# A new layout for the scratch that carries the query and key parts from one arrangement to another

## The reference

```python
def proj(W):
    return (X @ W.T).reshape(b, n, H, 2 * dh).transpose(0, 2, 1, 3)
Q, K, V = (proj(Wq), proj(Wk), proj(Wv))
Q1, Q2 = jnp.split(Q, 2, axis=-1)
K1, K2 = jnp.split(K, 2, axis=-1)
A1 = jnp.where(causal, jnp.einsum('bhnd,bhmd->bhnm', Q1, K1) * scaling, -jnp.inf)
A2 = jnp.where(causal, jnp.einsum('bhnd,bhmd->bhnm', Q2, K2) * scaling, -jnp.inf)
attn = jax.nn.softmax(A1, axis=-1) - lam * jax.nn.softmax(A2, axis=-1)
```

## Time and profile before

| | us |
|---|---|
| median of 3 runs | 543.09 |
| lowest and highest | 539.36, 544.16 |
| the profiled execution | 540.0 |
| its span in the profile | 538.0 |
| PE busy | 483.7 (90%) |
| DVE busy | 392.4 (73%) |
| ACT busy | 288.0 (54%) |
| POOL busy | 267.0 (50%) |

### The profile page before, as it was taken

How to read it: one execution, slowest core, us unless ns; L and a number is a source line. 1 busy time by engine, 2 the same in 40 slices (tenths; PEclk the granted TensorE clock), 3 DMA queues, 4 the chain that set the end, 5 groups by cost and what they waited for, 6 DMA issues and landing times.

```text
span 538.0 us, 8610 instructions
## 1 busy us (share of the span) xinstructions
PE 483.7 (90%) x3104; PEld 232.8 (43%) x3104; DVE 392.4 (73%) x796; ACT 288.0 (54%) x460; POOL 267.0 (50%) x223
## 2 busy tenths in 40 slices
PE   4892788888999999998997999999997998999995
PEld 4641443443445354453344545444343444443442
DVE  2414741969988988659887888469988977876584
ACT  1431444146686553656674654647773485548732
POOL 6031313124584914617653357626656467438963
PEclk9997789999999999999999999999999999999999
DMA  8700489803068480202486146111485166202111
GB/s 282 262 2 19 119 121 127 144 7 101 1 161 101 106 113 5 78 21 60 117 128 117 40 63 96 43 60 40 136 138 85 25 106 114 79 5 79 40 39 41
DMA packets 48474, 46.03 MB, mean 86 GB/s; under 512 B 5200, under 2 KB 38064, under 8 KB 47792
## 3 DMA queue, kind: packets, MB, share of 16 engines
q1 hardware_dynamic: 48432, 45.48, 41.0%
HBM read 37.47 MB, written 7.60 MB: 84 GB/s over the span
## 4 chain that ended last, share of the span: by engine, by line
PE 56%; DVE 15%; DMA 7%; SPq 7%; POOL 5%; ACT 4%; issue 4%; POOLq 1%; DVEq 0%; ACTq 0%
PE bank L737 7%; PE bank L728 6%; PE bank L749 6%; DMA ka<-parts_scratch 6%; PE scores L769 5%; SPq L514 5%; DVE nmax L1271 5%; PE scores L763 4%; PE bank L824 4%; PE scores L679 3%; PE scores L702 2%; PE scores L655 2%; PE scores L664 2%; PE scores L658 2%; PE bank L837 2%
## 5 line engine op out<-in xcount | busy, mean ns | idle before, releaser
L1070 POOL TENSOR_TENSOR gb<-gb,wb 128x512 f32<-128x512 f32 x64 | 84.7, 1324 | 114.8 <-ACT gb L978 104.2
L1271 DVE TENSOR_REDUCE nmax<-scores 128x4 f32<-128x1024 f32 (+1 forms) x96 | 113.7, 1216 | 32.2 <-PE scores L769 31.7
L1063 POOL TENSOR_SCALAR_AFFINE_SELECT pk<-pk 128x512 f32<-128x512 f32 (+1 forms) x96 | 82.9, 872 | 62.3 <-ACT pk L991 61.5
L991 ACT ACTIVATE pk<-scores 128x1024 f32<-128x1024 f32 x96 | 95.6, 1024 | 27.3 <-PE scores L769 27.1
L975 ACT ACTIVATE gt<-bank,bgh 128x512 f32<-128x512 f32 (+1 forms) x68 | 46.8, 688 | 62.6 <-PE bank L728 54.7
L737 PE MATMUL bank<-xnt,wu 128*128 128x512 f32 x128 | 69.2, 622 | 2.4 <-DVE h L1250 2.4
L728 PE MATMUL bank<-xnt,wg 128*128 128x512 f32 x128 | 68.7, 618 | 0.0
L749 PE MATMUL bank<-h,wd 128*128 128x512 f32 x128 | 66.8, 615 | 0.1
L1243 DVE SCALAR_TENSOR_TENSOR h<-gt,gb 128x512 f32<-128x512 f32 x64 | 49.6, 775 | 17.1 <-POOL gb L1070 12.6
L1250 DVE SCALAR_TENSOR_TENSOR h<-bank,bu,h 128x512 f32<-128x512 f32 x64 | 48.1, 751 | 17.3 <-PE bank L737 15.4
L763 PE MATMUL scores<-mask_h,ident_h 64*128 64x256 bf16 (+2 forms) x384 | 37.5, 273 | 12.3 <-DMA ka<-parts_scratch 8.2
(11 more groups left out here) (191 smaller groups left out, 732.3 us busy)
## 6 DMA issues: line engine op xcount, KB each, us to landing
wb<-wt_scratch SPq DMA_DIRECT2D x64, 256.0 KB, 4.1
parts_scratch<-parts SPq DMA_DIRECT2D x48, 128.0 KB, 2.4
qa<-parts_scratch SPq DMA_DIRECT2D x16, 192.0 KB
ka<-parts_scratch SPq DMA_DIRECT2D x16, 192.0 KB
qa<-parts_scratch SPq DMA_DIRECT2D x16, 128.0 KB
ka<-parts_scratch SPq DMA_DIRECT2D x16, 128.0 KB
x<-in_x SPq DMA_DIRECT2D x4, 256.0 KB, 2.7
ha<-in_wkq SPq DMA_DIRECT2D x1, 1024.0 KB, 5.2
```

The source lines that it names most:

```text
L991: A(dst.rearrange("p (h m) q -> p m h q", m=2), pairs[pair_of(step)][:, :, :].rearrange("p m (h q) -> p m h q", q=cols), ACT.Exp, scale=SC ...
L1063: pool.affine_select(out=dst, in_=dst, compare_op=ALU.is_ge, fill=0.0, base=0, pattern=[[0, heads], [1, P]], channel_multiplier=-1).then_i ...
L1070: pw(gb[:, c % 2, :], gb[:, c % 2, :], wb[:, k % 2, j % 2, :], ALU.mult).then_inc(s_ga_done, 1)
L1271: V.tensor_reduce(dst, src, AX, ALU.max, negate=True).then_inc(s_nmax_done, 1)
```

## The change

The scratch was laid out by chunk, q or k, head, component, term, dimension, token. It is now by chunk, q or k, batch, term, component, dimension, head, token. So the 16 heads x 256 tokens that a row of `qa` or `ka` takes lie in one run of 8 KB, where they were 16 runs of 512 B. For this the columns of `wq1` and `wk1` are put in order on the host, component first, then dimension, then head, so that tile f of a product holds component f. A tile that is stored is 128 rows of two runs of 512 B (one for each batch), where it was 128 rows of one run of 1 KB.

```diff
@@ step store
                                     r = a if n == 0 else 2 - a
                                     sp.wait_ge(done, at(c, name, 2 * n + f + 1))
-                                    dst = t["parts_dram"][c, n, f * 2 * GH:(f + 1) * 2 * GH, :, r * DH:(r + 1) * DH, :]
-                                    sp.dma_start(dst, parts[:, a, 2 * n + f, :]).then_inc(s_parts_stored, 16)
+                                    dst = t["parts_dram"][c, n, :, r, f * DH:(f + 1) * DH, :, :]
+                                    sp.dma_start(dst.rearrange("b d h t -> (d h) b t"),
+                                                 parts[:, a, 2 * n + f, :].rearrange("p (b t) -> p b t", b=CB)).then_inc(s_parts_stored, 16)
@@ step fetch
                                 for width in (3, 2, 1):
                                     first = 0 if n == 0 else 3 - width
-                                    src = t["parts_dram"][c, n, :, m, first * DH:(first + width) * DH, b * SEQ:(b + 1) * SEQ]
-                                    sp.dma_start(dst[row:row + width * DH, b, :, :],
-                                                 src.rearrange("h r t -> r h t")).then_inc(s_qk_in[b], 16)
+                                    src = t["parts_dram"][c, n, b, first:first + width, m * DH:(m + 1) * DH, :, :]
+                                    sp.dma_start(dst[row:row + width * DH, b, :, :], src).then_inc(s_qk_in[b], 16)
                                     row += width * DH
@@ the scratch
-    t["parts_dram"] = nc.dram_tensor("parts_scratch", (CHUNKS, 2, HEADS, 2, 3 * DH, CHUNK), BF16, kind="Internal").ap()
+    t["parts_dram"] = nc.dram_tensor("parts_scratch", (CHUNKS, 2, CB, 3, 2 * DH, HEADS, SEQ), BF16, kind="Internal").ap()
@@ the host
+    def rooms(w):
+
+        return w.reshape(P, HEADS, 2, DH).transpose(0, 2, 3, 1).reshape(P, -1)
-        "wq1": v["L1_attn_Wq"].T, "wk1": v["L1_attn_Wk"].T, "wv1": v["L1_attn_Wv"].T,
+        "wq1": rooms(v["L1_attn_Wq"].T), "wk1": rooms(v["L1_attn_Wk"].T), "wv1": v["L1_attn_Wv"].T,
```

## The result

The changed kernel takes 595.78 us (median of 4 runs, 594.58 to 596.47) against 543.62 us: a ratio of 1.097 with a 95% interval of 1.092 to 1.102. It is 52 us slower. I had said 30, with an upper end of 590: the way was right, the size and the range were not.

The account below looks back on a forecast made before the run. PE was taken to bound the kernel, five of eight fetches ending on its path. 27.1 + 1 + 1 + 4 - 3 = 30.1 us on 540.0 gave 570.1, plus 3 for the median: 573, range 555 to 590.

Parts of the forecast that it names:

- The mechanism: Fetches of ka: the smaller slowest count sets the engines, so the three DMA kinds use 3, 2 and 8.
- the five fetches on the path: Fetches 0/0, 1/0, 2/0, 3/0 and 3/1, each longer microsecond being one of PE's: +27.1 us together.
- the two with cover: Fetches 1/1 and 2/1, which had 24.2 and 24.3 us and need 23.5 to 24.5: +1 us for both.
- the stores: Stores to the scratch: 256 runs of 512 B for 128 of 1 KB, still 16 engines, +1 us.
- the clock: PE at half clock after four long waits, half of it counted: +4 us, between 0 and 14.
- the time of a fetch: Two engines carry 68 rows, 21.5 us at 25.9 GB/s, plus 2.0 fixed: 23.5 us from first issue.
- What comes back: Other engines drain their work while PE waits, so PE's idle 10% shrinks: -3 us, between 0 and -6.
- (c): Rival: wb parts queue behind fetches on the two engines, POOL's product L1070 waits longer, 585 to 590 us; chance 0.11.
- (a): Rival: fetches stay spread over the engines and long runs pay, so all four PE waits go, about 535 us; chance 0.06.
- (b): Rival: fetches stay spread but run length was never the limit, so nothing changes, 543 us; chance 0.09.

Follow-up runs that it names:

- the bare transfers: No kernel, only DMAs of 8 KB rows, each kind four times: 24 rows from 3 x 8 took 10.62 us, plain 24 rows 5.05 us.
- e1: Changed kernel with component ahead of term in the scratch, so a fetch's source rows lie together: 534.79 us, 0.981 of the original; second run 535.47 us, 0.979.
- e5: Changed kernel with 60 of the 64 wb loads left out: 578.89 us, ratio 1.065 to the kernel before the change.
- e4: Changed kernel with idle matmuls in front of PE's waits for the fetches: 586.72 us, ratio 1.076 to the kernel before the change.

## Why the prediction went wrong in size

- **The mechanism was right.** The source's 3 and 2 set the engines., one DMA of 24 KB, carried this; the shares 0.18 and 0.12 of the bare transfers and the 0.13 of the fetch show it, and e1 undoes it alone.
- **The sum.** In place of 27.1 for the five fetches on the path, 1 for the two with cover, 1 for the stores, 4 for the clock and -3, together 30.1, the profiles show 41.8 + 3.8 + 12.1 - 1.9 = 55.8; what the stores did is in the 41.8.
- **The step that failed first: the time of a fetch.** I took 23.5 us plus what lies ahead, 121.3 us for the five; they took 136.9, 15.6 more. I counted what the two engines have ahead, not what runs beside them: the `wb` loads that SP issues right behind a fetch. With only the first two `wb` steps left (e5) the five take 127.4, so 9.5 of the 15.6 go with the other loads, the few just ahead of a fetch among them. The other 6.1 stand in e5 too. 1.3 of them is 1/0, which took 24.8 with nothing beside it where my sum had 23.5, and 3.5 is 0/0, beside which fetch 0/1 and one `wb` step still run in e5; what 0/0 loses to which isn't shown.
- **Cover.** 1/1 and 2/1 wait for 0.57 and 3.25 us, 3.8 where I gave them 1 together; 2/1 too has `wb` loads beside it. On the other hand 1/0 costs 4.8 instead of 6.6. I said +1 for the stores and that nothing is gained by an SP that is sooner; but they got faster (2.0 us to landing instead of 2.4, their issue 463 ns instead of 597). From the first store's issue to the fetch's it is 7.8 us instead of 10.9, so that the fetch starts earlier before PE comes to its use: 20.0 us instead of 16.9. In 0/0 PE came 2.1 us sooner, which lengthened its wait.
- **The clock.** I gave 4 us, with 14 as the bound, because I thought that DVE's reductions hide half. It was 12.1 in PE's busy time, and e4 gets 9.1 of it back between medians and 12.9 in the profiled span. Little or nothing is hidden: behind the wait for 2/0 PE is busy without a gap from 315.5 to 323.
- **What comes back.** I took 3; it was 1.9.
- **The rivals.** (c) did not happen: POOL's wait for `wb` is 10.3 in one place, as before. I read it so that the loads come late for POOL only while PE is late as well; no run tests that. (a) and (b) can't hold for a source that is cut in 3. For one that isn't, e1 tells them apart: long runs shorten fetch 1/0 by some 12%, much nearer to (b), and the time comes out where (a) had it.
- **The range** was too narrow: the three large misses (the fetches, the two with cover, the clock) all went to the same side, and only the stores' term went to the other. The 3 us between the profiled execution before and its median, which I added, didn't come either: the changed kernel's profiled execution is its median.

The kernel with the rows together, at 0.979 (0.975 to 0.984), beats both. Of its gain of 9 to 11 us in the medians its profile shows 4.9 us of waits and a fetch of batch 0 that starts earlier. The two profiled executions are only 2.7 us apart in span (538.0 and 535.3), the one before the change with 540.0 one of its fastest, so the rest can't be placed by these traces.

## What to carry to other kernels

Look at the slowest count of both sides of a DMA before its length of run: a layout that makes runs 16 times as long and leaves 3 as the source's slowest count took twice the time in the bare transfers, and 8 rows put next to their like gave it back. A DMA share that stands for microseconds at a small multiple of 1/16 is the sign of it. And where PE comes to wait as long as here (4.8 to 12.5 us, five times), charge the half clock behind it in full, and charge the transfer with what is issued behind it, not only what lies ahead.

## What the runs showed that I had not expected

- SP's issue took longer where the two sides of a DMA had different shapes. Durations in ns (minimum, median, maximum) of the issues of `ka`, with sources of 3 x 8, 2 x 8 and 8 rows in the changed kernel:

```profile
L515 SPq DMA_DIRECT2D ka<-parts_scratch x48: 427/627/2979, 73.3 to 484.0; - x48
```

The same issues of e1_rows_together's second run, whose two sides have equal shapes, as many and as large:

```profile
L515 SPq DMA_DIRECT2D ka<-parts_scratch x48: 292/312/1901, 71.9 to 436.4; - x48
```

The median is half, 312 ns for 627. By kind it is some 700 ns for 24 rows, 627 for 16 and 432 for 8 in the changed kernel, and 293, 350 and 312 with the rows together. The 8 rows have equal shapes in both, so the shapes aren't all of it, and the number of engines changes along with them; no run takes the two apart. Stores have the same shape on both sides since the change too, and went from 597 to the 463 ns of this row:

```profile
L500 SPq DMA_DIRECT2D parts_scratch<-parts x48: 359/463/594, 53.9 to 423.5; - x48
```

- One engine alone moved 26.5 GB/s (53 GB/s on two), as much as each of 16 together (422 GB/s at a share of 1.02 in the earlier trace rows). Where 24 rows went over twelve engines, each got half of that: 156 GB/s.
